# The prologue of a four-layer graph kernel, put in another order

## What is computed

```python
x = _layernorm(x + _L0_gnn_ref(x, adj, W1, b1, W2, b2, fusion_w))        # 5 node groups, two graph convolutions each
x = _layernorm(x + _L1_gnn_ref(x, adj, Wq, Wk, Wv, Wo, bo))              # attention, 8 heads, log(adj) as bias
x = _layernorm(x + _L2_gnn_ref(x, adj, W, b))                            # one normalised graph convolution
x = _layernorm(x + _L3_gnn_ref(x, adj, nodemask, weight, w_ih, w_hh, b_ih, b_hh))  # 5 gated (GRU) steps
```

## Time and profile before

| | us |
|---|---|
| median of 3 runs | 1834.2 (1833.7 to 1834.89) |
| the profiled execution's own time | 1837.68 |
| its span, first to last instruction | 1835.6 |

### The profile page before, as it was taken

The page is one execution under the profiler, slowest core; times in us unless marked ns, Lnnn a source line. Parts: engine busy times, 40 slices in busy tenths (PEclk is TensorE's granted clock), DMA queues, the critical chain, the costliest instruction groups (busy, mean ns, idle before and its releaser), DMA issues.

```text
span 1835.6 us, 33530 instructions
## 1 busy us (share of the span) xinstructions
PE 1665.9 (91%) x12060; PEld 1365.6 (74%) x12060; DVE 1485.6 (81%) x3978; ACT 1187.1 (65%) x2738; POOL 733.4 (40%) x619
## 2 busy tenths in 40 slices
PE   3678999999998999999999999999999999999885
PEld 2466878787787877788787878778787878877763
DVE  3367797988979798897979889797978889797864
ACT  0345767667776766767676667767676676756662
POOL 1113353443445354343535344353534434443431
PEclk8688999999999999999999999999999999999997
DMA  2101010100001010100100010000101000000000
GB/s 71 33 10 30 1 39 13 28 24 19 21 13 39 13 28 24 28 13 14 38 13 27 24 27 24 14 27 13 31 21 28 24 16 25 13 24 12 12 7 11
DMA packets 84797, 40.89 MB, mean 22 GB/s; under 512 B 10629, under 2 KB 84634, under 8 KB 84634
## 3 DMA queue, kind: packets, MB, share of 16 engines
q1 hardware_dynamic: 84634, 38.77, 7.6%
HBM read 30.36 MB, written 8.39 MB: 21 GB/s over the span
## 4 chain that ended last, share of the span: by engine, by line
PE 60%; DVE 23%; ACT 11%; issue 3%; SPq 1%; POOL 0%; DMA 0%; DVEq 0%; POOLq 0%; ACTq 0%
PE RA L837 12%; PE RB L837 11%; PE Q L806 6%; PE RT L1007 6%; ACT e_s L514 5%; PE RT L806 4%; DVE stats L610 4%; PE Q L934 3%; PE Q L965 2%; PE M L876 2%; PE M L870 2%; DVE tr L779 2%; PE Q L949 2%; DVE mv L613 2%; PE Q L917 2%
## 5 line engine op out<-in xcount | busy, mean ns | idle before, releaser
L456 POOL TENSOR_TENSOR h_lo<-hT,h_hi 128x512 fp32r<-128x512 f32 x160 | 204.9, 1280 | 574.1 <-ACT h_hi L534 483.7
L514 ACT ACTIVATE e_s<-Q,s_ng 128x128 f32<-128x128 f32 x1024 | 297.0, 409 | 17.4 <-DVE s_ng L727 17.0
L424 POOL TENSOR_TENSOR rs<-ve,half_neg 128x4 f32<-128x4 f32 x128 | 148.5, 1160 | 321.3 <-DVE ve L615 321.3
L459 POOL TENSOR_TENSOR hd<-hT,nn 128x512 f32<-128x512 f32 x160 | 221.7, 1385 | 40.6 <-ACT nn L546 40.4
L727 DVE TENSOR_REDUCE s_ng<-Q 128x4 f32<-128x512 f32 x256 | 170.5, 683 | 17.0 <-PE Q L934 16.2
L540 ACT ACTIVATE tr<-RA,b_rz 128x512 f32<-128x512 f32 x160 | 114.8, 718 | 104.4 <-PE RA L837 104.4
L733 DVE TENSOR_TENSOR p_s<-Q,adjTe 128x512 f32<-128x512 f32 x256 | 172.3, 684 | 12.0 <-PE Q L806 11.7
L546 ACT ACTIVATE nn<-tr,wT 128x512 f32<-128x512 f32 x160 | 118.6, 741 | 88.0 <-DVE tr L779 86.9
L806 PE MATMUL Q<-ident,e_s 128*128 128x128 f32 x1024 | 156.4, 279 | 11.9 <-ACT e_s L514 11.8
L775 DVE SCALAR_TENSOR_TENSOR un<-tr,un 128x512 f32<-128x512 f32 x160 | 110.3, 689 | 63.9 <-ACT un L543 60.7
L837 PE MATMUL RB<-h_hi,whh_hi 128*128 128x512 f32 x320 | 145.7, 455 | 11.1 <-ACT tz L549 11.1
(11 more groups left out here) (187 smaller groups left out, 4190.8 us busy)
## 6 DMA issues: line engine op xcount, KB each, us to landing
adjn<-in_adj_dram SPq DMA_DIRECT2D x32, 256.0 KB, 2.9
xin<-in_x_dram SPq DMA_DIRECT2D x32, 256.0 KB, 3.3
adjr<-in_adj_dram SPq DMA_DIRECT2D x32, 256.0 KB, 3.2
out_dram<-x SPq DMA_DIRECT2D x32, 256.0 KB, 2.4
adjc<-in_adj_dram SPq DMA_DIRECT2D x128, 4.0 KB, 1.7
xs<-in_x_dram SPq DMA_DIRECT2D x128, 16.0 KB, 1.8
W1s<-in_L_gnn_W_dram SPq DMA_DIRECT2D x1, 640.0 KB
W2s<-in_L_gnn_W_dram SPq DMA_DIRECT2D x2, 320.0 KB
```

The costliest lines, as they stand in the source:

```text
L424: return pool.tensor_tensor(r[:, :], v[:, :], half_neg[:, 0, 0:GB], ALU.pow)
L456: pool.tensor_tensor(h_lo[g][:, :], hT[g][:, :], h_hi[g][:, :], ALU.subtract).then_inc(SG["h_lo"][g], 1)
L459: pool.tensor_tensor(hd[g][:, :], hT[g][:, :], nn[g][:, :], ALU.subtract).then_inc(SG["hd"][g], 1)
L514: ins = act.activation(e_s[:, j, c, :], Q[j][:, c * P:(c + 1) * P], ACT.Exp, bias=s_ng[:, j, c:c + 1])
```

## The change

The change touches only the prologue and the packed transfers. The packed inputs of iteration 0 are now loaded first: `adjc` from SP's queue, right behind fusion_w, and `xs` from ACT's queue. The bias pieces, W1s and W2s come next, and the other weights last, and each set has a semaphore of its own (`fw_in`, `bias_in` 4, `first_in` 3, `w_in` now 11 transfers). POOL signals `consts_ready` before it clears `z_t`, `f_t` and `vp`, and has `zeros_ready` for those. DVE does `l0_deg`, `l0_prep` and `l0_nat2` of iteration 0 before it copies the weights out. PE transposes the block with the biases alone at first, then does `l0_nat2` and `l0_y`, and takes the other 17 transposes between the two halves of `l0_hid` and the five products behind the second half. Waits for all weights now stand where a weight is first used. In later iterations the four `adjc` and four `xs` of a group are issued in blocks instead of in turn. The work of the body is the same.

```diff
-        def program(eng, engine, steps):
+        def program(eng, engine, steps, begun=()):
...
-                    if 0 <= it - lag < ITERS:
+                    if 0 <= it - lag < ITERS and not (it == 0 and kind in begun):
...
+            sp.dma_start(fw[:, :], fusion_w.partition_broadcast(P)).then_inc(fw_in, 16)
+            for g in range(NG):
+                load_packed_adj(sp, g, 0)
+            sp.wait_ge(w_pool, 1)
+            sp.dma_start(stage[0:10, BIAS, :], b1.rearrange("g (h p) -> (g h) p", p=P)).then_inc(bias_in, 16)
...
+            sp.dma_start(W1s[:, :, :], W1.rearrange("g d e -> d g e")).then_inc(first_in, 16)
...
             for i, w in enumerate((Wq, Wk, Wv, Wo, L2W)):
                 sp.dma_start(stage[:, i, :], w).then_inc(w_in, 16)
...
-            for t in (sel, z_t, f_t, vp[0]):
-                after(pool.memset(t[tuple([slice(None)] * len(t.shape))], 0.0))
-            pool.memset(vp[0][:, :, :, DH:DH + 1], 1.0)
+            after(pool.memset(sel[:, :, :], 0.0))
...
             pool.memset(half_neg[:, :, :], -0.5).then_inc(consts_ready, 1)
+            for t in (z_t, f_t, vp[0]):
+                after(pool.memset(t[tuple([slice(None)] * len(t.shape))], 0.0))
+            pool.memset(vp[0][:, :, :, DH:DH + 1], 1.0).then_inc(zeros_ready, 1)
...
+            for g in range(NG):
+                load_packed_x(act, g, 0)
             act.wait_ge(w_prep, 2)
             act.activation(fw[:, :], fwx[:, :], ACT.Exp).then_inc(w_exp, 1)
-            act.wait_ge(w_evac, 7)
...
+            steps(0, 0, "l0_deg", 0)
+            dve.wait_ge(w_exp, 1)
...
+            dve.wait_ge(w_mm, 1)
+            dve.tensor_copy(wT[:, BIAS, :], RA[:, 0:P]).then_inc(w_evac, 1)
...
+            steps(0, 0, "l0_prep", 0)
+            steps(0, 0, "l0_nat2", 0)
+            for i in range(5):
+                dve.wait_ge(w_mm, i + 2)
...
+            def turn_weights():
+
+                pe.wait_ge(w_in, 16 * WEIGHT_DMAS)
+                for i in range(17):
...
+            def multiply_weights():
+
+                pe.wait_ge(w_evac, 6)
...
+                    if it + k == 0:
+                        pe.wait_ge(first_in, 16 * FIRST_DMAS)
                     for c in range(NK):
                         ins = pe.matmul(group_cols(M2, c), W1s[:, c, k * P:(k + 1) * P], y_t[:, :, group_slots(c)], start=True, stop=True)
                     ins.then_inc(S["w1_mm"], 1)
+                    if it == 0:
+                        turn_weights() if k == 0 else multiply_weights()
...
+                    if it + g == 0:
+                        pe.wait_ge(w_evac, 8)
                     wait(pe, "x1", it, g + 1)
...
+            pe.wait_ge(consts_ready, 1)
+            pe.wait_ge(bias_in, 16 * BIAS_DMAS)
+            turn(RA[:, 0:P], stage[:, BIAS, :]).then_inc(w_mm, 1)
+            steps(0, 0, "l0_nat2", 0)
+            steps(0, 0, "l0_y", 0)
+            program(pe, "tensor", steps, ("l0_nat2", "l0_y"))
```

More of the change, by code:

```diff
@@ L319, in _ @@
             sp.dma_start(stage[:, MASK, :], nodemask).then_inc(w_in, 16)
[L320 to L327, removed]
             sp.dma_start(bo_row[:, :], bo.partition_broadcast(P)).then_inc(w_in, 16)
             sp.dma_start(l2b_row[:, :], L2b.partition_broadcast(P)).then_inc(w_in, 16)
-            sp.dma_start(fw[:, :], fusion_w.partition_broadcast(P)).then_inc(w_in, 16)
             def load_small(g, it):
[L333 to L340, removed]
+                if it == 0:
+                    return
+                wait(sp, "y_mm", it - 1, 1)
+                load_packed_adj(sp, g, it)
+                load_packed_x(sp, g, it)
             def load(g, it):
@@ L560, in after @@
                 dve.wait_ge(w_prep, n[0])
[L562 to L604, removed]
-            ins.then_inc(w_evac, 1)
             def moments(at, y, st, m, v):
@@ L799, in steps @@
                     normalise(x4[g], y4[g], mv4[g], rs4[g]).then_inc(SG["x4"][g], 1)
-            program(dve, "vector", steps)
+            dve.wait_ge(fw_in, 16)
+            after(dve.tensor_reduce(fw_s[:, 0:1], fw[:, :], AX_X, ALU.max))
+            after(dve.tensor_scalar(fwx[:, :], fw[:, :], fw_s[:, 0:1], None, ALU.subtract))
+            dve.wait_ge(consts_ready, 1)
+            after(dve.tensor_reduce(ident_small[:, :], ident[:, :].rearrange("p (b n) -> p n b", b=GB), AX_X, ALU.add))
+            after(dve.tensor_tensor(member_x[:, :, :], member[:, :, :],
+                                    ident_small[:, :].unsqueeze(1).broadcast_to([P, NK, NS]), ALU.mult))
@@ new lines, in _ @@
+            after(dve.tensor_reduce(member_p[:, :], member_x[:, :, :], AX_X, ALU.add))
+            after(dve.tensor_reduce(head_p[:, :], ident[:, :].rearrange("p (h r) -> p h r", h=HEADS), AX_X, ALU.add))
+            after(dve.tensor_reduce(slot_p[:, :], head_p[:, :].rearrange("p (a i) -> p i a", i=2), AX_X, ALU.add))
+            after(dve.tensor_reduce(block_p[:, :], ident[:, :].rearrange("p (b n) -> p b n", b=GB), AX_X, ALU.add))
+            for c in range(1, NK):
+                dve.tensor_reduce(grp[:, c:c + 1], ident_small[:, SLOT[c]:SLOT[c + 1]], AX_X, ALU.add).then_inc(w_prep, 1)
@@ new lines, in _ @@
+            n[0] += NK - 1
+            dve.wait_ge(w_prep, n[0])
+            for c in range(1, NK):
+                dve.tensor_copy(same[:, SLOT[c]:SLOT[c + 1]], grp[:, c:c + 1].broadcast_to([P, SLOT[c + 1] - SLOT[c]])).then_inc(w_prep, 1)
+            n[0] += NK - 1
+            dve.wait_ge(w_prep, n[0])
+            steps(0, 0, "l0_deg", 0)
+            dve.wait_ge(w_exp, 1)
+            after(dve.tensor_reduce(fw_s[:, 1:2], fw[:, :], AX_X, ALU.add))
+            after(dve.reciprocal(fw_s[:, 2:3], fw_s[:, 1:2]))
@@ new lines, in _ @@
+            after(dve.tensor_copy(whh_hi[:, :, :], wT[:, WHH:WHH + 3, :]))
+            dve.tensor_tensor(whh_lo[:, :, :], wT[:, WHH:WHH + 3, :], whh_hi[:, :, :], ALU.subtract).then_inc(w_evac, 1)
+            for i in range(LAYERS):
+                dve.wait_ge(w_mm, 7 + i)
+                product = [RA, RB, *Q][i][:, 0:3 * P]
+                after(dve.tensor_copy(comp_hi[:, i, :], product))
+                ins = dve.tensor_tensor(comp_lo[:, i, :], product, comp_hi[:, i, :], ALU.subtract)
+            ins.then_inc(w_evac, 1)
@@ L803, in _ @@
+            dve.wait_ge(zeros_ready, 1)
+            program(dve, "vector", steps, ("l0_deg", "l0_prep", "l0_nat2"))
         @block.tensor
```

59 lines of the change are left out of this document (45 added, 14 removed).

## The result

| | us |
|---|---|
| before, median of 4 runs | 1834.55 (1833.7 to 1835.33) |
| changed, median of 4 runs | 1810.19 (1807.31 to 1810.95) |
| ratio | 0.9863, 95% interval 0.9848 to 0.9877 |
| the changed kernel's profiled execution | 1810.14, span 1808.3 |

The kernel is 24.4 us faster (1.3%).

What follows compares the result with a forecast made beforehand. The body, mostly on PE, bounds the kernel, so only its start counts: 23.2 us earlier a_i less 7.7 of PE work gives 15.6, plus 2.6 from PE's clock, 18.2 less: 1834.2 to 1816.0 us, range 1811 to 1821.3.

Steps and rivals of the forecast that it cites:

- What bounds the kernel, and that SP moves along: Whole span: chain mostly on PE (60%), body unchanged; SP's transfers behind its deg_s wait move with the first layer.
- a_i at 6.9, bound by the tables: Prologue: first layer's first instruction begins at 6.9 us, 8 at latest, bound by DVE's tables; 23.2 us earlier.
- POOL's clears beside DVE's tables at nothing: Prologue: POOL's clears of z_t, f_t, vp beside DVE's tables cost nothing; bound one clear, under 1 us.
- Layer to l0_hid 10.8 us, biases hidden: First layer: a_i to l0_hid stays 10.8 us, l0_hid at 17.7; bias work hides in POOL's power, 0.4 us spare.
- Weights landed by 19.1: Prologue: all other weights land at about 19.1 us, 1.2 us ahead of the transposes' start at 20.3.
- rival B: Prologue inputs late: weights land behind 20.3 or a_i waits; up to 2.7 us, 1818.7 or 1821.3; chance 0.12.
- PE's clock: 2.6 us: First layer: clock rises during the five products, saving 0.3 to 1.6 us there and 2.4 in l0_z; 2.6 taken.
- 15.6: First layer: us by which l0_z begins earlier from order alone, 23.2 less 7.7 of PE work moved in.
- Own time and median: Whole run: profiled execution, 1837.68, lies 3.5 us above the runs' median; difference carried over, giving 1834.2 - 18.2 = 1816.0.
- the 23.2: Prologue: us by which a_i was to begin earlier, at 6.9 instead of 30.12.
- Rivals C and D: Behind l0_z: C, clock falls elsewhere, 1823.6, chance 0.05; D, PE stays at 1.2 GHz, 1845, chance 0.02.
- D: Slower: PE at 1.2 GHz through 63.4 us of work, 29 us lost; decides from about 22 lost; chance 0.02.

## Why the prediction was wrong, point by point

- **What bounds the kernel, and that SP moves along.** Right: the body's work kept its length (27.0 us of distance at iteration 2, 27.2 at iteration 15), and SP's wait for deg_s moved with the layer.
- **a_i at 6.9, bound by the tables.** Right: 6.96, with POOL's half_neg ending at 4.07 (forecast 4.06). The runs with the clears first and with one queue, where a_i came 2.1 and 3.1 us later, confirm both the bound and the second queue's worth. By the medians the second queue saves 2.3 to 2.6 us at the end, with intervals that overlap. The Trainium skill (DMA: Bandwidth & Descriptors, section "Issuing engines are not separate DMA queues") says that a second queue saves only time of issue, usually small beside the transfer. The trace agrees that it is time of issue that is saved, but with many small transfers that time isn't small: eight issues took 3.73 us, against some 2 us from one issue to its landing.
- **POOL's clears beside DVE's tables at nothing.** Right: from ident_small at 4.18 to the end of same at 6.93 are 2.75 us, against 2.74 alone. The four copies of same, of which the prediction feared a conflict with a clear, began at 6.54, and the last clear had ended at 6.17; so no run shows what the two do side by side.
- **Layer to l0_hid 10.8 us, biases hidden.** Right: 17.60 for 17.7.
- **Weights landed by 19.1.** Too late by some 2 us: where all engines waited for all weights in this order, they were there at 17.30, and in the changed kernel the last one, issued at 13.20, took 4.1 us to land. Nobody waited for them in the changed kernel; rival B did not occur.
- **PE's clock: 2.6 us. This is the step that failed.** The mechanism was named, and with the right sign, but its size was 8.6 us in the trace. The forecast let the clock rise during the five products, because there the trace of before had shown it rise. In the changed kernel it rose during the transposes, near 21.5 and in the second trace near 23, with PE at work since 17.6, so the five products (2.9 us), the second half of l0_hid (1.4), part of the transposes (1.3), l0_z (2.6, from 4.98 to 2.41 on the chain) and the next transposes (0.4) were quick. What is left for the order is 24.1 - 8.6 = 15.5, against 15.6. The term was also set under its own bounds: 0.3 to 1.6 for the products and 2.4 for l0_z make 2.7 to 4.0, and 2.6 was taken. But with 4.0 the forecast would have been 1814.6, still 4 us above the result, so that slip isn't what decided. What should have warned: my own sum had PE without a gap from 17.7 on, 9 us ahead of the first product, and I counted the gapless stretch from the products on only. The products before stood behind an idle gap of 2.9 us; what the clock did there says nothing on products that follow 9 us of unbroken work, and I carried it over as if it did.
- **Own time and median.** The profile of before is of an execution of 1837.68 us, 3.1 above the median. In it the last weight landed at 15.4. In the two other traces with the old order of transfers and of work (the runs with idle products) PE's first transpose began at 14.21 and 14.33. The difference is SP's stop at the first bias piece, 2.80 us in the trace of before and 1.53 and 1.75 in these two. The changed kernel doesn't wait for that landing: a_i began between 6.95 and 6.97 in each trace that has its prologue up to there. So a microsecond of the 23.2 belonged to that execution. Without it the forecast would have been a gain of 17.2, still further from the 24.4. The last 3 us of the 27.2 between the two traces came between the first layer's end and iteration 2, where the clock falls and rises several times. In the second trace of the changed kernel the power of iteration 2 began at 122.88 instead of 121.23. How much of these 3 us is the change's and how much the two executions' is open; the medians lie 24.4 us apart, close to the 24.1 at the first layer's end, and leave little for the change.
- **Rivals C and D** (gain given back by the clock) did not occur: the granted clock was 0.966 over the whole span, 0.956 before. Two readings under D don't hold, though neither is in the sum. A loss of 22 us is three quarters of 29 and not 60%, and would need a mean clock near 0.56 and not 0.60. And dense work did not raise the clock each time: l0_z's 4.98 us and the transposes from 15.49 to 19.5 ran at 1.2 GHz to their end in the trace of before.

## What to carry to other kernels

A sum of durations from a trace holds them at the clock they ran at there. When a change closes PE's gaps or moves work next to other work, ask anew where the clock rises, and count the whole unbroken stretch from its first instruction; price both levels for each term. Where a serial prologue runs on a mostly idle PE, idle products in its waits are a cheap test of what the clock is worth (8.9 us here in the old order), and work that must be done anyway, put into the gaps, does both. Transfers and the waits on them are to be moved together: the new order of work alone gave 10 us, the new order of transfers alone cost 3, and both gave 24.

## What the runs showed of the hardware that was not expected

- The granted clock reads 1.00 up to its first change, in every trace here (the first fall comes between the 22nd and the 68th microsecond), while in the changed kernel the same ten products take 2.61 us at 17.6 and 1.34 at 22.7. Up to the first fall only durations tell the level.
- The place of the clock's rise differs between executions of one kernel: near 21.5 and near 23 in the two traces of the changed kernel, whose two medians are 0.3 us apart. It went where PE's work went: to 25 with an idle gap of 1.37 us put ahead of the transposes, behind 33.4 where the whole layer came 13.4 us later, and ahead of the layer where idle products began at 4.11.
- A DMA issue from ACT takes what one from SP takes, 3.73 us for eight.
- SP stopped for 2.80, 1.53, 1.75 and 2.20 us at the first bias piece (5 KB) in the four traces in which it stands behind all the large weights. With W1s and W2s issued early the longest single issue of a weight was 0.70 to 0.93 us. A first packed transfer of iteration 1 (4 KB), behind two large inputs, took 2.00 us to issue in the trace of before, at 62.90, where the others took 0.42. What in the queue holds SP up is not shown.
